# Attention scores once, with the queries on the partitions and turned probabilities

## The reference, cut to what matters

```
x = x + 0.5 * ffn(layernorm(x), w_gate, w_up, w_down)
x = x + attn(layernorm(x), wq, wk, wv, wo)
x = x + 0.5 * ffn(layernorm(x), w_gate, w_up, w_down)

def attn(x, wq, wk, wv, wo):
    q, k, v = x @ wq.T, x @ wk.T, x @ wv.T          (heads apart; q and k rotated)
    scores = q @ k.T / sqrt(64)                     (-inf above the diagonal)
    probs = softmax(scores, axis=-1)
    return (probs @ v) @ wo.T
```

## Time and profile before

| | us |
|---|---|
| median of 3 runs | 1344.22 (1341.71 to 1344.45) |
| the profiled execution | 1344.47 |
| its span, first to last instruction | 1342.6 |

### The profile page before, as it was taken

How to read it: one execution, slowest core, us unless ns; L and a number is a source line. 1 busy time by engine, 2 the same in 40 slices (tenths; PEclk the granted TensorE clock), 3 DMA queues, 4 the chain that set the end, 5 groups by cost and what they waited for, 6 DMA issues and landing times. The chain is left out here.

```text
span 1342.6 us, 24933 instructions
## 1 busy us (share of the span) xinstructions
PE 1284.2 (96%) x6240; PEld 734.8 (55%) x6240; DVE 874.2 (65%) x2270; ACT 619.0 (46%) x1176; POOL 752.1 (56%) x454
## 2 busy tenths in 40 slices
PE   4986799999999999999999999999999999999798
PEld 2543455555555555555555556555655555554365
DVE  5566667676767666776767676767676767664254
ACT  3655244444444444444444444444444444444474
POOL 5133256666666666666666565666666666665300
PEclk8998689999999999999999999999999999999799
DMA  7123816464656565655556465646464646452001
GB/s 274 41 94 102 190 45 158 112 158 113 158 119 158 119 158 120 158 119 139 139 124 154 111 161 117 158 108 163 105 161 106 162 103 163 106 116 50 0 24 40
DMA packets 113340, 164.81 MB, mean 123 GB/s; under 512 B 13344, under 2 KB 63392, under 8 KB 113184
## 3 DMA queue, kind: packets, MB, share of 16 engines
q1 hardware_dynamic: 112832, 163.43, 47.8%
q10 hardware_dynamic: 480, 1.05, 0.4%
HBM read 36.24 MB, written 10.49 MB: 35 GB/s over the span
## 5 line engine op out<-in xcount | busy, mean ns | idle before, releaser
L979 POOL TENSOR_TENSOR psum_p<-psum_p,shared_a 128x256 f32<-128x256 f32 (+1 forms) x192 | 280.7, 1462 | 101.4 <-ACT shared_a L807 92.7
L807 ACT ACTIVATE shared_a<-bank 128x512 f32<-128x512 f32 (+3 forms) x512 | 201.5, 445 | 235.6 <-PE bank L662 228.0
L645 PE MATMUL bank<-k_hh,q_hl 128*128 128x512 f32 (+3 forms) x768 | 257.4, 390 | 11.0 <-DVE max_all L937 8.4
L662 PE MATMUL bank<-q_hm,k_l 65*128 65x512 f32 (+3 forms) x768 | 244.8, 373 | 0.0
L869 DVE TENSOR_REDUCE max_left<-bank 128x1 f32<-128x512 f32 x256 | 175.5, 688 | 96.8 <-PE bank L645 96.8
L656 PE MATMUL bank<-q_hl,k_hh 128*128 128x512 f32 (+3 forms) x768 | 227.5, 350 | 6.7 <-DMA q_hm<-neg_max_rows 6.7
L645 PEld LDWEIGHTS bank<-k_hh,q_hl 128*128 128x128 f32 x768 | 138.2, 193 | 174.7 <-issue 73.7
L807 ACT ACTIVATE probs_more<-bank 128x512 f32<-128x512 f32 (+1 forms) x256 | 132.2, 568 | 195.5 <-PE bank L662 182.5
L873 DVE CUSTOM_DVE_ANT_0 max_scratch<-bank,tri_mask,max_left 128x128 f32<-128x128 f32 (+3 forms) x256 | 138.1, 548 | 109.4 <-PE bank L645 109.0
L682 PE MATMUL bank<-shared_a,v_cur 128*64 128x512 f32 (+3 forms) x1024 | 202.7, 474 | 0.0
L103 POOL TENSOR_TENSOR parts<-rotated,parts 128x1024 fp32r<-128x1024 f32 x64 | 152.4, 2381 | 50.3 <-ACT parts L97 50.3
(11 more groups left out here) (128 smaller groups left out, 1919.1 us busy)
## 6 DMA issues: line engine op xcount, KB each, us to landing
q_hl<-parts SPq DMA_DIRECT2D x254, 128.0 KB, 2.8
k_hh<-parts SPq DMA_DIRECT2D x254, 128.0 KB, 2.7
v_cur<-shared_b SPq DMA_DIRECT2D x32, 512.0 KB, 6.0
k_l<-parts SPq DMA_DIRECT2D x63, 256.0 KB, 4.2
q_hm<-parts SPq DMA_DIRECT2D x63, 256.0 KB, 4.9
xn_cur<-xn_scratch SPq DMA_DIRECT2D x15, 1024.0 KB, 5.8
w_qk<-w_scratch SPq DMA_DIRECT2D x32, 256.0 KB, 3.1
w_scratch<-first_w_parts SPq DMA_DIRECT2D x8, 512.0 KB, 3.1
```

What stands on the lines that cost most here:

```text
L645: nc.tensor.matmul(max_bank[k % 2][:, 0:w], q_hl[u][h][:, q * P:(q + 1) * P], k_hh[u][h][:, keys * CHUNK:keys * CHUNK + w], start=True, st ...
L662: nc.tensor.matmul(scores[h][:, x0:], k_l1[u][h][:, keys], q_hm[u][h][:, q], start=False, stop=True).then_inc(scores_full, 1)
L807: nc.scalar.activation(probs_of(s)[:, h, x0:], scores[h][:, x0:], ACT.Exp, scale=SCORE_SCALE).then_inc(probs_done, 1)
L979: last = nc.gpsimd.tensor_tensor(acc, acc, new, ALU.add)
```

## The change

Attention is written anew around one computation of the scores. The loops over pairs, the projections, the product with V in fp32 and the output projection stay; the layout of scores and probabilities changes.

- The 8 query tiles of 128 of each head are split into two groups (`TILES`: tiles 0, 1, 6, 7 and tiles 2, 3, 4, 5), each with 18 key blocks of 128. For every head and query tile (`UNITS`, 16 a pair), `score` computes one row of scores, queries on the partitions, up to 1024 columns wide: a product with `k_hh` and one with `k_low` per up to 512 columns. `k_low` has 128 rows, the lower 64 are zero. There are two tiles of 1024 columns in PSUM (`wide_banks`), used in turn.
- The tables of cosine and sine hold the factor -1/8 for the queries, so the scores come out negated. DVE (`max_of`) adds the mask (+1e30), writes the masked scores to `probs` in SBUF and takes the minimum of the row in the same instruction (`neg_max`).
- ACT (`exponential`) computes exp in place in SBUF, with the row's minimum as bias, and the sum of the row by the instruction's accumulator (`sums`).
- TensorE transposes the probabilities in blocks of 128 (`turn`, 10 calls a group), into two PSUM banks used in turn (`ring`); ACT copies them to SBUF (`keep_turned`), four slots in `turned`. `times_v` then takes two key blocks a call, 7 calls a pair. One PSUM bank (`out_bank`) serves both groups.
- The sums: DVE takes the reciprocal of 8 numbers a partition (`invert`), POOL spreads it over 512 columns (`spread`), TensorE turns it (`turn_sums`, 4 transposes), ACT copies it (`keep_sums`), DVE multiplies (`normalise`).
- The rotation: DVE writes four products (`terms`, `cross`); their sum (`sum_half`), the high part and the low part are made by POOL (`rope_half`). There is one tile `rotated` in place of two.
- Gone are `max_unit`, the mask matmul, `sum_probs`, `add_probs`, Ln and Exp of the sums, `round_half` on ACT within the loop, `send_max`, and the copy of the queries to `q_hm`.

The core of the diff:

```diff
-            def max_unit(p, i, u, k):
...
-                    nc.tensor.transpose(max_bank[k % 2][:, 0:P], max_all[c][:], ident[:]).then_inc(max_full, 1)
...
-            def score(p, i, u, s):
...
+            def score(p, i, u, g, k):
+                h, r = UNITS[k]
...
+                if some(unit(p, g, k) - 2):
+                    pe.wait_ge(scores_taken, unit(p, g, k) - 2)
+                q = q_hl[u][h][:, P * TILES[g][r]:P * (TILES[g][r] + 1)]
+                x0, x1 = scores_at(g, k)
+                for a, b in ((x0, min(x1, CHUNK)), (CHUNK, x1)):
+                    if b > a:
+                        out, keys = wide_banks[k % 2][:, a:b], slice(a - x0, b - x0)
+                        nc.tensor.matmul(out, q, k_hh[u][h][:, keys], start=True, stop=False)
+                        last = nc.tensor.matmul(out, q, k_low[u][h][:, keys], start=False, stop=True)
+                last.then_inc(scores_full, 1)
...
+            def turn(p, g, t, signals=1):
+                j, heads = TURNS[g][t]
+                at, rows = RING[g][t], rows_at(g, j)
+                if t < 2:
+                    pe.wait_ge(probs_done, unit(p, g, 4 * t + 3))
+                may_write(p, at)
+                for a, h in enumerate(heads):
+                    for b, r in enumerate(rows):
+                        col = P * (a * len(rows) + b)
+                        last = nc.tensor.transpose(ring[at % 2][:, col:col + P],
+                                                   probs[g][:, h, OFFSET[g][r] + j * P:OFFSET[g][r] + (j + 1) * P], ident[:])
+                last.then_inc(ring_full, signals)
...
-            def sum_probs(p, c):
...
+            def exponential(p, g, k):
+                h, r = UNITS[k]
+                col = slice(2 * r + h, 2 * r + h + 1)
+                act.wait_ge(scores_taken, unit(p, g, k))
+                settle(act)
+                own = part_of_probs(g, k)
+                nc.scalar.activation(own, own, ACT.Exp, bias=neg_max[g][:, col], scale=-1.0,
+                                     accum_out=sums[g][:, col]).then_inc(probs_done, 1)
...
+            def keep_turned(p, u, g, t, signals=1):
...
+                nc.scalar.activation(turned[:, slot, to], ring[at % 2][:, 0:w * len(heads)],
+                                     ACT.Copy).then_inc(ring_free[at % 2], signals)
...
+            def max_of(p, g, k):
...
+                dve.wait_ge(scores_full, unit(p, g, k))
+                if k == 0 and some(p):
+                    dve.wait_ge(ring_full, ring_count(p - 1, RING[g][9]))
+                x0, x1 = scores_at(g, k)
+                settle(dve)
+                nc.vector.tensor_tensor_reduce(out=part_of_probs(g, k), in0=wide_banks[k % 2][:, x0:x1],
+                                               in1=tri_mask[:, SEQ - (x1 - x0):], scale=1.0, scalar=3e38, op0=ALU.add,
+                                               op1=ALU.min, accum_out=neg_max[g][:, col]).then_inc(scores_taken, 1)
...
+            def rope_half(p2, u, c, ahead=False):
...
+                sum_half(nc.gpsimd, o)
...
+                nc.gpsimd.tensor_copy(o.parts[:, 0, :, cols], o.rotated[:]).then_inc(high_done, 1)
...
+                low_half(nc, o, c)
```

More of the change, by code:

```diff
@@ L7 @@
 F32R = mybir.dt.float32r
-BF16 = mybir.dt.bfloat16
 INT32 = mybir.dt.int32
@@ new lines, in turn_sums, with project_out @@
+            def turn_sums(p, g):
+                at = RING_SUM[g]
+                pe.wait_ge(inv_spread, 2 * p + g + 1)
+                may_write(p, at)
+                for r in range(4):
+                    last = nc.tensor.transpose(ring[at % 2][:, P * r:P * (r + 1)],
+                                               inv_wide[:, 2 * r:2 * r + 2, :].rearrange("p h d -> p (h d)"), ident[:])
+                last.then_inc(ring_full, 1)
+            def project_out(p, i, u, g, at, of):
+                if g == 0:
@@ L747, in _, with ahead, ahead_v, next_score @@
-            pe.wait_ge(zeros_done, 2)
-            for k in range(4):
-                max_unit(0, 0, 0, k)
+                def ahead(n):
+                    if has_next2:
+                        project(i + 1, u, n)
+                def ahead_v(n):
+                    if has_next2 and u == 0:
+                        project_v(i + 1, n)
+                def next_score(k):
+                    if has_next:
+                        score(p + 1, i + u, 1 - u, 0, k)
+                turn(p, 0, 0)
@@ L820, in pair, with keep_sums @@
+            def keep_sums(p, g):
+                at = RING_SUM[g]
+                act.wait_ge(ring_full, ring_count(p, at))
+                if some(2 * p + g):
+                    act.wait_ge(head_done, 2 * p + g)
+                nc.scalar.activation(inv_sum[:], ring[at % 2][:], ACT.Copy).then_inc(ring_free[at % 2], 1)
             def pair(i, u, first, last):
                 p = 2 * i + u
-                has_prev, has_next2 = not (first and u == 0), not last
-                for s in range(NS):
-                    for h in range(2):
-                        exponentials(p, s, h)
-                    if s in ROUND_AT and has_next2:
-                        round_high(i + 1, u, ROUND_AT[s])
-                    if s == 2 and has_prev:
-                        invert(p - 1, 1)
-                    if s == 6:
-                        invert(p, 0)
-                    if (u, s) in V_AT and has_next2:
-                        keep_v(i + 1, V_AT[u, s], 16 * (i + 1), 16 * (i + 1))
@@ L835, in _, with ahead_v, next_exponential @@
-            act.wait_ge(proj_free, 6)
+                has_prev, has_next, has_next2 = not (first and u == 0), not (last and u == 1), not last
+                def ahead_v(n):
+                    if has_next2 and u == 0:
+                        keep_v(i + 1, n, 16 * (i + 1))
+                def next_exponential(k):
+                    if has_next:
+                        exponential(p + 1, 0, k)
+                exponential(p, 0, 7)
+                keep_turned(p, u, 0, 0)
+                keep_turned(p, u, 0, 1)
@@ L843, in _ @@
                 keep_first_v(n)
-            for c in range(2):
-                round_high(0, 1, c, ahead=True)
+            for k in range(7):
+                exponential(0, 0, k)
             for u in range(2):
@@ L944, in _ @@
+            for k in range(2):
+                max_of(0, 0, k)
+            for n in range(3, 6):
+                rope(0, 1, n, ahead=True)
+                for k in (2 * n - 4, 2 * n - 3):
+                    max_of(0, 0, k)
             for u in range(2):
@@ L982, in pair, with spread @@
+            def spread(p, g):
+                pool.wait_ge(inv_done, 2 * p + g + 1)
+                if g == 1:
+                    pool.wait_ge(ring_full, ring_count(p, RING_SUM[0]))
+                elif some(p):
+                    pool.wait_ge(ring_full, ring_count(p - 1, RING_SUM[1]))
+                settle(pool)
+                nc.gpsimd.tensor_copy(inv_wide[:], inv[g][:].unsqueeze(2).to_broadcast([P, 8, HEAD_DIM])).then_inc(inv_spread, 1)
             def pair(i, u, last):
                 p = 2 * i + u
-                for s in range(NS):
-                    if s in LOW_AT and not last:
-                        split_low(i + 1, u, LOW_AT[s])
-                    add_probs(p, s)
@@ L1116, in macaron @@
         w_v = sb("w_v", [P, 2, 256], F32R)
-        banks = [ctx.enter_context(nc.psum_tensor(f"bank{i}", [P, CHUNK], F32)) for i in range(8)]
+        wide_banks = [ctx.enter_context(nc.psum_tensor(f"wide{i}", [P, SEQ], F32)) for i in range(2)]
+        banks = [w[:, k * CHUNK:(k + 1) * CHUNK] for w in wide_banks for k in range(2)]
+        banks += [ctx.enter_context(nc.psum_tensor(f"bank{i}", [P, CHUNK], F32))[:] for i in range(4, 8)]
         def sem(name):
```

679 lines of the change are left out of this document (320 added, 359 removed).

## The result

| | before | after |
|---|---|---|
| median | 1344.06 (1341.71 to 1344.45, 4 runs) | **1325.13** (1323.93 to 1327.55, 4 runs) |
| profiled execution, own time / span | 1344.47 / 1342.6 | 1324.65 / 1322.9 |

The ratio is 0.9865, 95% interval 0.9847 to 0.9883: faster by 1.35%, 19 us. The forecast was 79 us. The sign and the range held, three quarters of the size did not.

The account below looks back on a forecast made before the run. TensorE, never idle in the steady stretch, was taken as the bound: a pair falls from 34.5 to 32.1 us, so 32 pairs save 77 us and the ends 3, off 1344.5: 1265 us, range 1222 to 1360.

Parts of the forecast that it names:

- The ends: Start and end of the kernel outside the steady pairs: 4 us less at the end, 1 more at the start, 3 saved.
- Two transposes in a row ... I take 0.06: TensorE's price per transpose, chosen between bounds of 0.05 and 0.13: 80 x 0.06 = 4.8 us a pair.
- Changes of kind ... Together 4.0: TensorE's extra cost when switching between fp32, fp32r and transposes: 4.0 us a pair, on top of 28.2.
- behind a transpose group: Part of the switching cost on TensorE: fp32r work after a group of transposes, about 17 times at 0.07, 1.2 us a pair.
- leaving fp32: Part of the switching cost on TensorE: 9 first matmuls after fp32, 0.11 late each, 1.0 us a pair.
- Scores, product, projections, output: TensorE's work beside transposes, us a pair: scores 8.7, product with V 8.5, output 1.9, projections 2.9 and 1.4.
- ACT: Exponentials and copies, 20.4 us of 32 a pair, with something for reading 16 accumulators; from 46% to 64% busy.
- DVE and POOL: Both keep up with TensorE: DVE 18.7 us a pair, down from 23.8; POOL under 17.
- The tightest place: Beginning of group 1: TensorE 5.5 us against ACT's 4.7; costed at nothing, otherwise some 0.3 us a time.
- Transposes in a row are dear: Rival, slower: 58 transposes following another take 0.11 each, 35.0 us a pair, 1358 us; chance 0.12.
- The clock falls: Rival, slower: transposes lower TensorE's granted clock, a pair takes 35.3 us, 1368 us in all; chance 0.07.
- The lists wait: Rival, smaller gain: engines wait for each other, four or five waits of 0.3 us, 33.4 a pair, 1307 us; chance 0.21.

Follow-up runs that it names:

- x1: Every transposition of a block of probabilities issued twice, 72 more a pair, against the changed kernel: 1556.89 us, 232 more.
- x9: Kernel before the change, each of its two transpositions a pair (row maxima) issued four times in a row: 1363.09 us, 20 us more.
- x3: Changed kernel with exponentials written as bf16 and the probabilities transposed as bf16, widened again by ACT's copy: 1263.6 us, ratio 0.9404.
- x7: Changed kernel with fp32 transpositions, the exponentials not adding up their rows, so without ACT's 16 accumulator reads a pair: 1321.51 us.
- x13: Changed kernel with the last unit of scores on TensorE ahead of the transpositions of group 1's sums: 1319.38 us.
- x2: Changed kernel with only the first transposition of each call of turn kept, 20 a pair in place of 72: 1237.85 us.

## Why the prediction was wrong

**The frame was right.** TensorE's list is the path at full clock and nothing else takes its place: the change is worth what it takes off that list, and the four other engines have room. The pair was forecast at 32.1 and took 33.94: 1.8 x 32 = 59 us, which is the whole miss of 60. The ends came as put: 1344.5 - 32 x 34.40 = 243.7 before, 1324.65 - 32 x 33.94 = 238.6 after, 5 less where 3 were forecast.

**The step that failed is "Two transposes in a row ... I take 0.06".** It is 0.109, in the change, in x1, and in the kernel before (x9). 80 x 0.049 is 3.9 us a pair, 125 us. The choice was argued from the length of one weight load, 0.14 against 0.21; but the records of loads overlap, and four of them last 0.46 (the timeline in the section on the result), 0.11 for each further one. A record's length was read as its price, the very reading the text had ruled out for matmuls. The bound of 0.05 came from the next start, 0.05 after the transposition's; what that start gains, the second start loses.
The Trainium skill, "TensorE: Matmul & The Clock Gate", section "LDWEIGHTS (loading the stationary operand)", gives the time of a load as the number of its columns over 1.2, in ns: 107 for 128 columns, 53 for 64. The runs agree: 0.109 to 0.112 and 0.060. By that rule alone the forecast's sum would have been, as an estimate, 3.8 us a pair longer (80 x 0.047), 35.9. The next section of that page of the Trainium skill, "Weight-path perf modes — Fast Weight Load (FWL) and DoubleRow", says that the faster way of loading is not for fp32; x3's 0.056 beside 0.109 agrees.

**A second term hid half of it.** "Changes of kind ... Together 4.0" was too much. By the table, all work beside transpositions is 25.84 us; the forecast's bare terms for it are 23.4, and 0.55 is the wait before L680 (L637 to L680 takes 0.31 and 1.02 in turn, where 0.12 is the rest). That leaves 1.9, of which 1.5 (17.5 groups that an fp32r product follows, x 0.085) is the rest of a slot that begins on the transpositions' line. That line has 8.1; of it some 0.7 are changes of kind, since the second transposition behind a product with V starts 0.165 after the first and not 0.109 (6.5 a pair), and the entry from a transposition into such a product takes 0.202 (4 a pair). Slots at 80 x 0.109 = 8.7, bare work 23.4, true changes of kind 1.3, the wait 0.55: 33.9. Seen from the forecast's 32.2: 3.9 more for the slots, 2.7 less for changes of kind, 0.55 for the wait. Of those 2.7, 1.05 are slot: the 17 x 0.07 "behind a transpose group" and the 4 at 0.15 held 0.05 each of the missing part, counted for groups and not for members. The largest other part is leaving fp32, put at 0.11 for nine first matmuls: a transposition behind a product with V costs 0.056, behind an output projection nothing.

**Scores, product, projections, output** at bare prices: right within the above; the 128-column fp32r row that the earlier trace rows lacks, taken as 0.11, measures 0.11.

**ACT** at 20.4 us a pair took 24.9: the accumulator read, dismissed as "something", is 3.1, and exponentials over SBUF take 0.1 more than plain passes. By x7 the reads cost the change 3.6 us, which is not clear of noise (the intervals overlap). **DVE and POOL**: below, as forecast. **The tightest place** was named as the beginning of group 1, priced at nothing: right (L653 waited 0.2 us there in 1000). The wait that did exist was not foreseen: the sums' transpositions behind an addition on DVE.

**The rivals.** *Transposes in a row are dear* was the true mechanism, at the right price of 0.11, given 0.12. It came out at 1358 and not 1325 because it stood on the 4.0 of changes of kind; its turning point, "from a step of 0.10 on", fell with them. *The clock falls*: refuted by x1. *The lists wait* (1307) is nearest to the measured time, by its number alone: 0.55 us a pair were waits, 18 us where it had 42, by x13 only 6 of them to be had; the mechanism is real but shows in full only with shorter lists (30.8 us in x3, 28.4 in x2, waits taken off).
The Trainium skill, "TensorE: Matmul & The Clock Gate", section "Part 4: PE-mode transpose", says that transposes do not engage the full clock. No stretch here has transpositions alone; with 152 of them, 16 of 41 us, between matmuls (x1) the granted clock stays at 1.00. The 275 ns that this section of the Trainium skill gives is refuted as a price: one more in a row costs 0.109 us.

**How it could have been had.** x9 shows that no run of the change was needed, but also that the trace before had no two transpositions in a row. Between ends of 0.05 and 0.13 the one row that priced a whole transposition was the one at 0.13, and the text took a value by the other end by argument.

## What to carry to other kernels

Price a TensorE instruction by the distances around it, over two starts and not one, and ask what it loads as well as what it passes: here short products with 128 columns of new 4-byte weights cost 0.11 us each however little they pass, and bf16 transpositions half of that. When the list of the bounding engine is cut by a tenth or more, expect part of it back as waits between lists that had been hidden: here it was a third to a half (1.2 of 3.1 us a pair in x3, 2.8 of 5.5 in x2). Fill a wait with work that is ready; a step moved ahead of its data holds up all that is queued behind it.

## What the runs showed of the hardware

- A transposition and an fp32r product with 128 columns of 4-byte weights have nearly the same slot, 0.109 and 0.112 us; the bf16 transposition has 0.056, the fp32r product with 64 columns loaded 0.060, with 64 columns passed 0.112.
- After the last transposition of a group the next fp32r product starts 0.028 us later, and the one after it 0.085 late, with fp32 and with bf16 transpositions alike (the change, x3).
- ACT's reading of a row sum is an instruction of 0.19 us; DVE's is 0.08.
- The granted clock stays at the 2.4 GHz level with 16 of 41 us spent in transpositions between matmuls (x1).
- fp32 products with V have two records a matmul and 8.9 us a pair, bf16 ones have one and 3.5.
